# Attention block: the maxima of a query tile over all keys in one pair of PSUM banks

## The reference

```
x_n = _group_norm(x, gn_w, gn_b)
q = _conv1x1(x_n, wq, bq); k = _conv1x1(x_n, wk, bk); v = _conv1x1(x_n, wv, bv)
attn = softmax(einsum('bhqd,bhkd->bhqk', q, k) * hd ** -0.5)
out = einsum('bhqk,bhkd->bhqd', attn, v)
return x + _conv1x1(out, wp, bp)
```

## Time and profile before

| | us |
|---|---|
| Runs (three) | 396.8, 397.02, 398.1; median 397.02 |
| The profiled execution, its own time | 398.07 |
| Its span, first to last instruction | 396.2 |
| TensorE busy | 368.2 (93%) |
| ScalarE busy | 304.6 (77%) |
| VectorE busy | 303.2 (77%) |
| GpSimd busy | 258.9 (65%) |

### The profile page before, as it was taken

One profiled execution on the slowest core, in us unless ns is written; L12 is line 12 of the kernel. 1 busy time (PEld: TensorE's weight loads), 2 busy tenths in 40 slices (PEclk: granted clock), 3 DMA queues, 4 the chain that ended last, 5 costly groups with the idle time before them and its releaser, 6 DMA issues.

```text
span 396.2 us, 11202 instructions
## 1 busy us (share of the span) xinstructions
PE 368.2 (93%) x4625; PEld 228.9 (58%) x4625; DVE 303.2 (77%) x528; ACT 304.6 (77%) x352; POOL 258.9 (65%) x219
## 2 busy tenths in 40 slices
PE   1998899999999999999999999999999989999977
PEld 1743566556655557456665557556665646655554
DVE  4778988868887868868877977867877776988543
ACT  1747889978787779977888779978787877788850
POOL 5045865888397865879297866869477854549730
PEclk9999999999999999999999999999999999999999
DMA  6054600345510711234510721104521541131013
GB/s 212 7 132 128 154 10 2 81 124 75 151 28 19 195 31 55 71 91 92 146 48 15 160 83 55 28 3 95 100 101 28 120 123 56 23 114 29 2 28 108
DMA packets 31019, 30.92 MB, mean 78 GB/s; under 512 B 18796, under 2 KB 21112, under 8 KB 30968
## 3 DMA queue, kind: packets, MB, share of 16 engines
q1 hardware_dynamic: 30944, 30.19, 29.7%
q10 hardware_dynamic: 24, 0.01, 0.0%
HBM read 9.44 MB, written 4.19 MB: 34 GB/s over the span
## 4 chain that ended last, share of the span: by engine, by line
PE 61%; DVE 18%; ACT 7%; issue 5%; DMA 3%; POOL 2%; DVEq 1%; SPq 1%; POOLq 1%
PE gen L480 15%; PE st L551 8%; PE st L552 8%; PE mx L529 8%; DVE mx L806 8%; PE pv L569 5%; DVE p_lo L830 5%; PE pv L572 5%; PE pv L571 5%; PE st L480 2%; ACT st L742 2%; DMA oT_lo<-o_lo 2%; ACT xin L758 2%; ACT p_hi L739 2%; DVEq L801 1%
## 5 line engine op out<-in xcount | busy, mean ns | idle before, releaser
L806 DVE TENSOR_REDUCE mx<-mx 128x1 f32<-128x512 f32 x256 | 170.9, 685 | 31.3 <-PE mx L529 27.9
L739 ACT ACTIVATE p_hi<-st 128x1024 f16<-128x1024 f32 x128 | 131.2, 1025 | 61.3 <-PE st L552 59.5
L1023 POOL TENSOR_TENSOR p_lo<-p,p_hi 128x1024 f16<-128x1024 f32 x63 | 134.2, 2130 | 62.1 <-ACT p L742 61.9
L569 PE MATMUL pv<-v_hi,p_hi 128*128 128x65 f16 x1024 | 105.8, 194 | 3.1 <-DVE o L838 2.6
L572 PE MATMUL pv<-v_hi,p_lo 128*128 128x65 f16 x1024 | 105.9, 194 | 0.0
L571 PE MATMUL pv<-v_lo,p_hi 128*128 128x64 f16 x1024 | 105.9, 193 | 0.0
L569 PEld LDWEIGHTS pv<-v_hi,p_hi 128*128 128x128 f16 x1024 | 94.5, 98 | 13.7 <-issue 5.6
L571 PEld LDWEIGHTS pv<-v_lo,p_hi 128*128 128x128 f16 x1024 | 93.6, 98 | 13.7
L551 PE MATMUL st<-q_twice,k_both 128*128 128x512 f16 x256 | 97.0, 379 | 4.8 <-DVE p_lo L830 3.4
L552 PE MATMUL st<-q_max,k_one 65*128 65x512 f16 x256 | 97.2, 380 | 0.0
L572 PEld LDWEIGHTS pv<-v_hi,p_lo 128*128 128x128 f16 x1024 | 93.7, 97 | 0.0
(11 more groups left out here) (166 smaller groups left out, 493.1 us busy)
## 6 DMA issues: line engine op xcount, KB each, us to landing
xres<-in_x_dram SPq DMA_DIRECT2D x4, 1024.0 KB, 5.1
q_twice<-st_hi_q SPq DMA_DIRECT2D x28, 128.0 KB, 2.4
out_dram<-y SPq DMA_DIRECT2D x14, 256.0 KB, 2.4
xin<-in_x_dram SPq DMA_DIRECT2D x6, 512.0 KB, 4.4
k_both<-st_hi_k SPq DMA_DIRECT2D x16, 128.0 KB, 2.3
k_one<-st_hi_k SPq DMA_DIRECT2D x16, 128.0 KB, 2.3
k_both<-st_lo_k SPq DMA_DIRECT2D x16, 128.0 KB, 2.3
q_max<-st_lo_q SPq DMA_DIRECT2D x14, 128.0 KB, 2.4
```

Source lines behind the costliest of these rows:

```text
L569: nc.tensor.matmul(pv_v[:, q, :], hi, vh, start=k == 0 and q == 0, stop=False, skip_group_check=True)
L739: nc.scalar.activation(p_hi[:, G % PR, :, :], scores, ACT.Exp, scale=SM_SCALE / M_SCALE)
L806: nc.vector.reduce_max(mx8[:, U % 2, tile, part:part + 1], mxb[(MXJ * U + j) % 2][:, :], AX.X)\
L1023: nc.gpsimd.tensor_tensor(p_lo[:, G % PR, :, :], p_full(G), p_hi[:, G % PR, :, :], ALU.subtract)\
```

## The change

The two banks `mx0` and `mx1` become one tensor `mxb` of two banks. `maximum(U, tile)` now issues both matmuls of a query tile one after the other (all 1024 keys), and VectorE reduces all 1024 columns by one instruction. The four tiles of a unit stand in its four slots, one each, right behind the scores and ahead of any job. The join, the transpose on TensorE and its eviction are gone. VectorE scales the 128x4 maxima to fp16 (`row_shift`), right behind the fourth tile's reduction, and SyncE copies them straight to the row of `q_max`. To make that a plain copy, a tile is now every fourth query (`tile_of`), so the weights of these matmuls are read with a step of four elements. The shift's copy moves from the slots with G % 4 == 2 to those with G % 4 == 1, at the head of SyncE's slot. `pv` and `gen` become the two halves of a pair `pg`, which unit 0's tiles 0 and 2 use in the start-up. The low part of a v tile now stands ahead of the maximum on VectorE.

```diff
-    MAX_MIDWAY = ((), (), (), (2, 3), (6, 7), (MXJ - 1,))
-    MAX_AFTER = ((), (), (0, 1), (4, 5), (), ())
+    MAX_MIDWAY = ((), (), (), (1,), (3,), ())
+    MAX_AFTER = ((), (), (0,), (2,), (), ())
...
-        mxb = [pb("mx0"), pb("mx1")]
-        pv = pb("pv")
-        gen = pb("gen")
+        mxb = pb("mxb", 2)
+        pg = pb("pg", 2)
+        pv = pg[:, 0:512]
+        gen = pg[:, 512:1024]
...
+            U, tile = divmod(G + MX_AHEAD, SPU)
+            return (U, tile) if U < B * UNITS else None
+        def max_bank(n):
+            return (pg if n in (0, 2) else mxb), (n - 1 if n < QT else n)
+        def tile_of(half, tile):
+            return slice(half * HALF + tile, (half + 1) * HALF, QT)
...
-                wait(sp, s_mx_free, MXJ * (U + 1))
-                sp.dma_start(q_max[D:D + 1, head, halves(half)], shift_row[:, U % 2, :]).then_inc(s_shift_dma, 16)
+                wait(sp, s_shift, U + 1)
+                sp.dma_start(q_max[D:D + 1, head, halves(half)], shift[:, U % 2, :]).then_inc(s_shift_dma, 16)
...
-                U = shift_at(G)
-                if U is not None:
-                    shift_to_row(U)
+                top = maxima_at(G)
+                if top and top[1] == QT - 1:
+                    shift_to_row(top[0])
...
+            def maximum(U, tile):
                 _, head, half = unit(U)
+                bank, free = max_bank(QT * U + tile)
+                wait(pe, s_mx_free, free)
+                for j in range(2):
+                    last = nc.tensor.matmul(bank[:, halves(j)], q_twice[:, head, tile_of(half, tile)],
+                                            k_both[:, head, halves(j)], start=True, stop=True)
+                last.then_inc(s_mx_full, 1)
...
-                if done is not None:
-                    shift_transpose(done)
...
-                    maximum(U, n)
-                if todo and not early:
+                    maximum(U, tile)
+                if todo:
                     job(*todo)
-                if done is not None and old is not None:
-                    weigh(old)
-                if top:
-                    maximum(U, n + 1)
-                if done is None and old is not None:
+                if old is not None:
                     weigh(old)
...
+            def row_max(U, tile):
+                n = QT * U + tile
                 wait(dve, s_mx_full, n + 1)
+                nc.vector.reduce_max(mx[:, U % 2, tile:tile + 1], max_bank(n)[0][:, :], AX.X).then_inc(s_mx_free, 1)
+            def row_shift(U):
+                wait(dve, s_mx_free, QT * (U + 1))
                 wait(dve, s_shift_dma, 16 * (U - 1))
+                nc.vector.tensor_scalar(shift[:, U % 2, :], mx[:, U % 2, :], -1.0 / M_SCALE, P_LOG / SM_SCALE,
+                                        ALU.mult, ALU.add).then_inc(s_shift, 1)
...
-                wait_hi(pe, "k", j // QT + 1)
+                wait_hi(pe, "k", 2)
```

More of the change, by code:

```diff
@@ L522, in job @@
                     held.append((kind, i, j, b))
-            def maximum(U, j):
+            def maximum(U, tile):
                 _, head, half = unit(U)
-                wait(pe, s_mx_free, MXJ * U + j - 1)
-                tile, part = mx_part(U, j)
-                q = half * HALF + tile * P
-                nc.tensor.matmul(mxb[(MXJ * U + j) % 2][:, :], q_twice[:, head, q:q + P], k_both[:, head, halves(part)],
-                                 start=True, stop=True).then_inc(s_mx_full, 1)
-            def shift_transpose(U):
-                n = MXJ * U + MXJ - 1
-                wait(pe, s_mx_free, n - 1)
-                wait(pe, s_shift, U + 1)
-                nc.tensor.transpose(mxb[n % 2][0:QT, 0:P], mx4[:, U % 2, :], ident[:, :]).then_inc(s_mx_full, 1)
+                bank, free = max_bank(QT * U + tile)
[4 more added lines that the diff above has]
+                last.then_inc(s_mx_full, 1)
             def scores(G):
@@ L608, in transpose_weights, with first_maximum @@
                 last.then_inc(s_wT, 1)
-            def first_maximum(U, j):
-                half, rows = halves(j // QT), slice(U * D, (U + 1) * D)
+            def first_maximum(U, tile):
+                rows = slice(U * D, (U + 1) * D)
+                bank, free = max_bank(QT * U + tile)
                 wait_hi(pe, "q", 1)
-                wait_hi(pe, "k", j // QT + 1)
-                wait(pe, s_mx_free, MXJ * U + j - 1)
-                q = j % QT * P
-                nc.tensor.matmul(mxb[(MXJ * U + j) % 2][:, :], kq_hi["q"][rows, q:q + P], kq_hi["k"][rows, half],
-                                 start=True, stop=True).then_inc(s_mx_full, 1)
+                wait_hi(pe, "k", 2)
+                wait(pe, s_mx_free, free)
+                for j in range(2):
+                    last = nc.tensor.matmul(bank[:, halves(j)], kq_hi["q"][rows, tile_of(0, tile)],
+                                            kq_hi["k"][rows, halves(j)], start=True, stop=True)
+                last.then_inc(s_mx_full, 1)
             pe.wait_ge(s_const, 2)
@@ L650, in _ @@
             job("v", 0, 0, 0)
-            for j in range(2, 4):
-                first_maximum(1, j)
+            first_maximum(1, 1)
             pe.wait_ge(s_e32["k"], 3)
@@ L686, in _ @@
                 weigh(G)
-            job("y", 1, 0, B - 1, mxb[0])
+            job("y", 1, 0, B - 1, mxb[:, 0:512])
             weigh(TOTAL - 1)
@@ L793, in _ @@
                 slot(G)
[L794 removed]
+            for n, bank in enumerate((gen, mxb[:, 512:1024])):
                 tail_high(n, bank)
@@ L947, in _ @@
             nc.vector.tensor_tensor(bv_lo[:, :], bv_o[:, :], bv_hi[:, :], ALU.subtract).then_inc(s_bv, 1)
-            for j in range(MXJ - 1):
-                row_max(0, j)
-            join_max(0)
-            row_out(0)
-            for j in range(2):
-                row_max(1, j)
+            for tile in range(QT):
+                row_max(0, tile)
+            row_shift(0)
+            row_max(1, 0)
             dve.wait_ge(s_wpbv, 1)
@@ L956, in _ @@
                                            in1=vec["p"], op0=ALU.mult, op1=ALU.add).then_inc(s_bias_y, 1)
-            for j in range(2, 4):
-                row_max(1, j)
+            row_max(1, 1)
             low("v", 0, 0, 0)
@@ L965, in _ @@
             normalise(B * UNITS - 1)
-            finish(1, 1, mxb[0], halves(0))
-            for n, bank in enumerate((gen, mxb[1])):
+            finish(1, 1, mxb[:, 0:512], halves(0))
+            for n, bank in enumerate((gen, mxb[:, 512:1024])):
                 tail_low(n, bank)
```

76 lines of the change are left out of this document (18 added, 58 removed).

## The result

The changed kernel takes 406.31 us (median, 404.34 to 407.4) against 397.23 us (396.8 to 398.1) for the kernel before on the same chip: a ratio of 1.0218, interval 1.0185 to 1.025. The forecast was 396.7 us, within 392.5 to 400.5. The profiled execution took 407.4 us with a span of 405.7; the span of before was 396.2.

A forecast was written before the change was run, and what follows sets the result against it. TensorE was taken to bound about half the slots, the others waiting, mainly on VectorE. Span 396.2 - 5.3 + 0.1 + 4.95 = 395.95, profiled 397.8, 0.3 less than before; from the median 397.02, 396.7 us, range 392.5 to 400.5.

The forecast's parts named there:

- What is lost: SyncE's queue at g = 21 and 22: shift ahead of k's duplicates delays q's; 1.85, 1.85 and 1.25, sum 4.95 us.
- scaling to 2.89: In slot 21, VectorE's scaling of the maxima follows the reduction ending at 2.72 and ends 2.89 us into the slot.
- g = 10 to 13: Slots with v jobs: 9.12 us becomes 8.76 with one order, gaining 0.36 in each image, 1.44 us.
- The reductions and their order: VectorE: 128 reductions at 1.22 us replace pairs, 0.07 less per tile; a run of four falls from 9.23 to 8.83 us.
- The rival with 1.37 us: A two-bank reduction costs 1.37 us, runs of four 8.99, gain some 1 us less: 397.7 us; chance 0.08.
- k's six entries as long as q's six: SyncE's queue behind the shift: k's six duplicates take 3.82 + 0.05 us.
- That the queue doesn't hold TensorE: Shift to last duplicate takes under 10.7 us, not 13.0: 391.3 us, chance 0.15; in part, 393 to 395.8, 0.17.
- That short runs make the shift's copy slow: The shift's copy of 8-byte runs queues 1.27 us and ends slower: 398.6 up to 404 us; chance 0.24.
- The weights: Maxima's weights read in steps of four: zero taken, up to 12 us possible; rival 409 us, chance 0.04.
- The start-up: First tile needs both halves of k, so the first maximum goes from 19.89 to 20.83; 0.1 us lost.
- The forecast fails if a wait that I do not list appears, above all one for the pair of banks: Failure sign in the profile after: an unlisted wait, above all for the pair, now one buffer and not two.
- Slower: Slower by over 0.3%: chance 0.26, of it 0.22 for the slow shift copy and 0.04 for uncovered step-four weights.

The follow-up runs named there:

- without the hold: Changed kernel with the shift written by a VectorE reduction over one element, its constant in a 66th row of k_one and q_max: 402.68 us, ratio 1.0162.
- with the queue mended: Changed kernel with k's duplicates issued before the shift's copy, and the shift written by a one-element reduction, constant in a 66th row: 395.7 us, ratio 0.9969.
- the first run: Changed kernel with one move: at slot 21 SyncE issues the next image's k duplicates before the shift's copy, not behind it: 397.01 us, ratio 0.998.
- with the filling: Changed kernel with 14 useless matmuls into the free pair at slot 26, before the maximum that waits for the duplicates: 405.93 us, ratio 1.0248.

## Why the prediction was wrong

Two steps of it failed. The larger is the size of "What is lost", 4.95 us where 11.58 were measured: its mechanism was right, but one entry of the queue was taken too short (3.7 us in three images), and the clock behind the wait (3.3 us) wasn't in the sum. The other is "scaling to 2.89", 0.17 us for an instruction that can be held for 1.94, and it took 2.9 us of the gain. The move of the queue alone gave back 9.3 us, and the shift's instruction gone as well brought the time to 391.27.

Its gains against what the slots show, in us from slot 0 on (the last column is the changed kernel without the hold, outside g = 21 to 27):

| place | predicted | changed kernel | without the hold |
|---|---|---|---|
| image 4, slots 112 to 124 | 0.95 | 0.81 | 0.81 |
| g = 10 to 13 | 1.44 | 1.02 | 1.03 |
| g = 13 to 16, images 1 to 3 | 0 | -1.38 | -0.01 |
| g = 13 to 16, image 4 | 0.54 | 0.52 | 0.51 |
| wait for `normalise` at g = 16 | 0.12 | 0.18 | 0.19 |
| g = 0 to 10, images 2 to 4 | 0.99 | -0.47 | 1.23 |
| image 1, slots 0 to 10 | 0.85 | 1.27 | 1.08 |
| g = 17 to 20 and 28 to 31 | 0.42 | 0.33 | 0.31 |
| sum | 5.3 | 2.3 | 5.2 |
| g = 21 to 27, images 1 to 3 | -4.95 | -11.58 | |

- **The reductions and their order.** Right, but for one slot. 1219 ns for the forecast 1.22. The first two runs of four took 8.89 and 8.84 us (8.83 forecast; slot starts below), the third 8.89 against 8.96 before. g = 10 to 13 gained 0.33 to 0.35 in three images, and nothing in the first, whose slot 10 took 3.72 us against 3.37 in the others. There the maximum waits for the single pair (the third line below): in the first image slot 9 has no job, so TensorE is back before VectorE, which did a p_lo first, has reduced the tile before. It starts 0.34 us late, and that is the whole difference. The rival with 1.37 us is refuted.

```profile
364.68 0.38 PE L537 MATMUL st<-q_twice,k_both 128*128 128x512 f16 x1
373.52 0.38 PE L537 MATMUL st<-q_twice,k_both 128*128 128x512 f16 x1
```
```profile
56.48 0.60 PE L520 MATMUL mxb<-k_both,q_twice 128*128 128x512 f16 x2 [0.17 <-DVE mx L785]
```

- **The scaling.** Failed: 0.17 us for `row_shift` wherever it stands. It was taken as an instruction of VectorE like any other. The old one read PSUM; the new one reads and writes SBUF, and the prediction has no row of that kind beside GpSimd's work. Measured: 0.17 or up to 1.94, 21.4 us in all in place of 5.5, and 2.9 us on the path (5.6 with the queue mended). The Trainium skill (page "SBUF — State Buffer", section "Who interferes with whom") has the rule: a `tensor_scalar` whose operands meet certain conditions, within SBUF, can take the port pair that VectorE shares with GpSimd, whichever starts first holds it to its end and the other stands still, and on trn2 a `tensor_reduce` never contends. Both halves agree with the trace: 1.85 us ending 0.03 behind p_lo, and 156 to 158 ns in all 32 by reduction. One of the 32 in the changed kernel doesn't fit: beside a GpSimd `tensor_scalar` that had started first it took 0.45 us and ended 1.73 us ahead of it (the two lines below). It was a rule that spoke against this change, and the prediction didn't weigh it.
```profile
370.11 0.45 DVE L791 TENSOR_SCALAR shift<-mx 128x4 f16<-128x4 f32 x1
369.43 2.86 POOL L979 TENSOR_SCALAR xres<-xres,bias_y 128x1024 f32<-128x1024 f32 x1
```
- **The queue at g = 21 and 22.** Failed in size. The mechanism, the place and the issue of the shift (2.96 into the slot) were right. Slots 21 to 26 lost 2.80, 3.14 and 2.91 us, slot 27 1.68, 0 and 1.05, together 11.58 for 4.95. Of the 6.6 between, 3.7 are one entry: k_one's pair took 2.33, 2.68 and 2.45 us where "k's six entries as long as q's six" had q's 1.25. Another 3.3 are the clock behind the wait (2.73 in slot 27, 0.58 in slot 26 of image 3), for which the sum had no term. The other entries and the landing give back the 0.4 that is too much. A lengthened wait on a TensorE that is otherwise full is to be priced with what follows it.
- **The rivals.** That the queue doesn't hold TensorE: refuted, by the wait and by the first run. That short runs make the shift's copy slow: refuted; its entry took 494 ns (0.64 before) and it landed in 1.9 us at the median, 3.4 at most, with 2.4 and 4.2 for all the DMAs into q_max in the earlier trace rows. What the prediction took from the Trainium skill (page "DMA: Bandwidth & Descriptors", section "Why small descriptors are slow (HBM only)"), that copies within SBUF are spared that penalty, agrees with these. No row has the old copy's landing by itself. The weights: 18 ns each, 0 us in the time; the step is there in the load, and the sum stays as forecast.
- **The start-up** lost 0.25 us for the 0.1 taken.
- **The chances.** "The forecast fails if a wait that I do not list appears, above all one for the pair of banks" came true in its first half. The second half came true only in small: the maxima do wait for the pair, but what was lost by it against the kernel before came from the instruction that held VectorE, and the single buffer itself can be seen to cost 0.34 us in slot 10 of the first image. Slower had 0.26, on rivals that were all refuted; the range ended 5.8 us short.

Left open: why an entry of the queue takes 0.7 to 1.4 us more now and then within a burst of entries. It came once or twice from g = 21 to 26 of each image in the changed kernel and with the filling, and more rarely in the kernel before (its second transpose at 93.99 us of the first image took 2.01). So the short runs can't be the only cause, but what is wasn't tried. Open too is what the single pair costs elsewhere.

## What to carry to other kernels

Before moving a small multiply-and-add of VectorE from PSUM to SBUF, see which of GpSimd's long instructions it will stand beside, and price it at the rest of that instruction (up to 1.94 us here), with everything queued behind it on VectorE; the form that reduces took 0.16 us in all 32 places. When a copy that waits is put ahead of copies that don't, count the whole queue behind it, to the last landing; moving six entries ahead of one here gave back 9.3 us. And a mend can bring the same fault back elsewhere: look at the start of the first slot, not only at the steady part.

## What was not expected of the hardware

- A 128x4 multiply-and-add within SBUF took 0.17 to 1.94 us; the nine long ones ended 0.02 to 0.03 us behind GpSimd's p_lo; at the start, two of 512 columns took 3.15 us beside a 3.50 us memset on one partition row, and 0.99 alone.
- After 2.87 and 3.00 us of idle time TensorE's granted clock fell to 0.50 (1.2 GHz) for some 3.4 us, and after 3.21 us in another place it stayed at 1.00; matmuls of no use in the wait kept it at 1.00 in all three.
- A copy of 128 runs of 8 bytes within SBUF took 0.49 us in the queue and landed in 1.9 us, no later than the 128 KB copies beside it (2.4).
- Weights in steps of four 16-bit values loaded in 115 ns, not 97.
